# Order of transfers in one DMA queue of an adjacency-masked attention kernel: key factors and output transposes ahead of the probabilities' transposes

## What is computed

```
h    = relu(layernorm(x))                       # 4096 x 512
q    = h @ Wq.T + bq;  k = key @ Wk.T + bk;  v = value @ Wv.T + bv
s    = (q @ k.T) / 64 * adj                     # 4096 x 4096
s    = where(abs(s) < 1e-5, -1e9, s)
out  = x + (softmax(s) @ v) @ Wm.T + bm
```

## Time and profile before

| what | value |
|---|---|
| median of three runs | 1658.34 us (1650.92, 1658.34, 1658.66) |
| the profiled execution | 1648.3 us, of which its span is 1646.5 us |
| PE busy | 1534.5 us, 93% of the span, 6998 matmuls |
| DVE busy | 1135.8 us, 69% |
| ACT busy | 649.8 us, 39% |
| DMA queue of SP | 305.74 MB, 71.9% of 16 engines' time |
| mean granted TensorE clock | 0.988 of full speed |

### The profile page before, as it was taken

One profiled execution on the slowest core, in us unless ns is written; L12 is line 12 of the kernel. 1 busy time (PEld: TensorE's weight loads), 2 busy tenths in 40 slices (PEclk: granted clock), 3 DMA queues, 4 the chain that ended last, 5 costly groups with the idle time before them and its releaser, 6 DMA issues.

```text
span 1646.5 us, 23808 instructions
## 1 busy us (share of the span) xinstructions
PE 1534.5 (93%) x6998; PEld 692.3 (42%) x6998; DVE 1135.8 (69%) x2295; ACT 649.8 (39%) x1080; POOL 217.1 (13%) x291
## 2 busy tenths in 40 slices
PE   8998999959999999898999989899998989989898
PEld 5543444424334444343444434344443434434344
DVE  5889777747777666585766768576676857667573
ACT  5866444323333333343333434333343433334332
POOL 6163000010010101001010100101001010100100
PEclk9999999979999999999999999999999999999999
DMA  9725777757877778696776768677677867768664
GB/s 347 259 60 121 197 193 179 176 156 173 195 189 189 214 180 192 192 203 188 179 196 184 198 193 208 181 178 189 183 199 198 199 177 177 189 186 195 188 144 103
DMA packets 470020, 306.50 MB, mean 186 GB/s; under 512 B 378307, under 2 KB 390851, under 8 KB 469830
## 3 DMA queue, kind: packets, MB, share of 16 engines
q1 hardware_dynamic: 469952, 305.74, 71.9%
q10 hardware_dynamic: 6, 0.01, 0.0%
HBM read 194.78 MB, written 19.40 MB: 130 GB/s over the span
## 4 chain that ended last, share of the span: by engine, by line
PE 71%; DMA 14%; DVE 6%; SPq 5%; issue 3%; ACT 2%; DVEq 0%; ACTq 0%
PE R L871 11%; PE R L872 11%; PE R L873 11%; DMA Kbuf<-key_factors 11%; PE S L871 9%; PE S L873 8%; PE S L872 8%; SPq L593 4%; PE M L871 3%; PE M L872 3%; PE M L873 3%; DMA ho<-row 1%; PE R L989 1%; DVE Zbuf L1657 1%; DMA key_factors<-early 1%
## 5 line engine op out<-in xcount | busy, mean ns | idle before, releaser
L1335 ACT ACTIVATE drop<-Zbuf 128x512 f32<-128x512 f32 x256 | 160.8, 628 | 663.3 <-DVE cmx L1657 351.5
L871 PE MATMUL R<-Vbuf,pT 128*128 128x512 f16 x1008 | 384.6, 382 | 4.9 <-DMA pT<-ph 2.3
L872 PE MATMUL R<-Vbuf,pT 128*128 128x512 f16 x1008 | 384.5, 381 | 0.0
L873 PE MATMUL R<-Vbuf,pT 128*128 128x512 f16 x1008 | 384.1, 381 | 0.0
L871 PE MATMUL S<-Kbuf,qT 128*128 128x512 f16 x628 | 239.9, 382 | 66.4 <-DMA Kbuf<-key_factors 66.0
L873 PE MATMUL S<-Kbuf,qT 128*128 128x512 f16 x628 | 240.2, 382 | 0.0
L872 PE MATMUL S<-Kbuf,qT 128*128 128x512 f16 x628 | 239.9, 382 | 0.0
L1713 DVE SCALAR_TENSOR_TENSOR Zbuf<-S,rs,adjb 128x512 f32<-128x512 f32 x145 | 108.5, 748 | 117.8 <-PE S L873 103.6
L1657 DVE CUSTOM_DVE_ANT_0 Zbuf<-drop,Zbuf 128x512 f32<-128x512 f32 x256 | 183.7, 718 | 0.0
L1765 DVE TENSOR_SCALAR drop<-drop,common 128x512 f32<-128x512 f32 x232 | 135.8, 585 | 64.4 <-ACT drop L1335 62.2
L871 PEld LDWEIGHTS R<-Vbuf,pT 128*128 128x128 f16 x1008 | 98.8, 98 | 127.6 <-DMA pT<-ph 4.7
(11 more groups left out here) (277 smaller groups left out, 2048.0 us busy)
## 6 DMA issues: line engine op xcount, KB each, us to landing
Kbuf<-key_factors SPq DMA_DIRECT2D x171, 512.0 KB, 4.1
adjb<-in_adj_dram SPq DMA_DIRECT2D x256, 256.0 KB, 3.4
xq<-in_x_dram SPq DMA_DIRECT2D x32, 256.0 KB, 2.9
Kbuf<-in_L_gnn_key_dram SPq DMA_DIRECT2D x8, 1024.0 KB, 13.9
xr<-in_x_dram SPq DMA_DIRECT2D x32, 256.0 KB, 2.8
out_dram<-xr SPq DMA_DIRECT2D x31, 256.0 KB, 3.1
Vbuf<-in_L_gnn_value_dram SPq DMA_DIRECT2D x7, 1024.0 KB, 7.8
key_factors<-early SPq DMA_DIRECT2D x48, 128.0 KB, 2.4
```

Source lines behind the costliest of these rows:

```text
L871: nc.tensor.matmul(ps, lhs[0], rhs[0], start=start, stop=False, skip_group_check=added)
L872: nc.tensor.matmul(ps, lhs[0], rhs[1], start=False, stop=False, skip_group_check=added)
L873: return nc.tensor.matmul(ps, lhs[1], rhs[0], start=False, stop=stop, skip_group_check=added)
L1335: nc.scalar.activation(drop[:, :], tile_of(s.i, s.j), ACT.Abs).then_inc(abs_ready, 1)
```

## The change

In SP's `step` the inner loads move from behind the probabilities' transpose to ahead of it, and the transpose of a finished row's output moves from the end of the step to a place right behind the inner load. Each keeps its own waits. Nothing is added or left out on any engine. `turn_out` is the old text of the output's transpose as a function.

```diff
@@ -580,6 +580,14 @@
+            def turn_out(s, rows):
+                wait(sp, o_split, s.b - 1)
+                sp.sem_inc(split_seen, 1)
+                if s.has_next:
+                    wait(sp, qp_done, s.b + 2)
+                    sp.sem_inc(slot_seen, 1)
+                sp.dma_start_transpose(ho[:, :, :, :].rearrange("p h s n -> p (h s) n"), rows).then_inc(o_in, 16)
+
             def load_probs(s):
                 u = s.j - LAG_P
                 wait(sp, p_lo, s.t - LAG_P + 1)
@@ -603,15 +611,17 @@
                     sp.wait_ge(kt_stored, 16 * (2 * len(PIECES) if s.three else 32))
                     wait(sp, scores_done, s.t)
                     load_factor(*starts[s.j])
+                inner = INNER_THREE if s.three else INNER_TWO
+                if s.strassen and s.j in inner:
+                    if s.j == 4 or s.j == 6:
+                        wait(sp, unit_mm, 2 * s.before + s.j - 2)
+                    else:
+                        wait(sp, p1_mm, s.before + {2: 1, 3: 2, 5: 3}[s.j])
+                    load_factor(*inner[s.j])
+                if s.c == 4 and s.has_out and not last_out(s):
+                    turn_out(s, rows)
                 if s.early:
                     load_probs(s)
-                    inner = INNER_THREE if s.three else INNER_TWO
-                    if s.j in inner:
-                        if s.j == 4 or s.j == 6:
-                            wait(sp, unit_mm, 2 * s.before + s.j - 2)
-                        else:
-                            wait(sp, p1_mm, s.before + {2: 1, 3: 2, 5: 3}[s.j])
-                        load_factor(*inner[s.j])
                 if s.has_scores and s.more_adj:
 
                     wait(sp, z1_ready, s.t + 1)
@@ -627,13 +637,6 @@
...
-                if s.c == 4 and s.has_out and not last_out(s):
-                    wait(sp, o_split, s.b - 1)
-                    sp.sem_inc(split_seen, 1)
-                    if s.has_next:
-                        wait(sp, qp_done, s.b + 2)
-                        sp.sem_inc(slot_seen, 1)
-                    sp.dma_start_transpose(ho[:, :, :, :].rearrange("p h s n -> p (h s) n"), rows).then_inc(o_in, 16)
```

## The result

The changed kernel took 1591.74 us in the median of four runs (1588.81 to 1592.98), the kernel before 1654.72 beside it (1650.92 to 1658.66). The ratio is 0.9617 with a 95% interval of 0.9583 to 0.9651, so 3.8% faster. The forecast was 1596 us, with a range of 1576 to 1625. The profiled executions went from a span of 1646.5 to 1591.2 us, 55.3 us less, against a sum of 58.

The account below looks back on a forecast made before the run. PE was taken to be bound by 83.3 us of waits for key factors, mostly inner loads late in SP's queue. Gains of 55, 2.0 and 1 us sum to 58; 1654 - 58 = 1596 us, range 1576 to 1625.

Parts of the forecast that it names:

- a sum of 58: Total predicted gain in us: 55 from eleven passes with three units, 2.0 in pass 4, 1 in pass 3.
- The bound and the cause: PE waits 83.3 us for factors; in steps 3 to 6 inner loads are late by SP's queue order, not transfer length.
- the two gaps of pass 3: PE waits of 8.6 and 8.1 us, each ending with a first B11 whose load stays behind the transpose.
- What is late next: Steps 3 to 6: ACT's copies and DVE's sums limit the gain; 23.8 us a pass, 5.0 gained, eleven passes 55.
- all gaps close: Rival: DVE and ACT early enough, steps 3 to 6 fall to 21.3 us a pass, 87 us gained, 1567 us; chance 0.06.
- The output's transpose, costed at nothing: Moving 31 output transposes in SP's queue gains nothing, as PE reads `ho` only at the end of step 6.
- Passes 3 and 4: Pass 4 gains 2.0 us from its first two gaps, pass 3 gains 1 us from an earlier load.
- Head loads: Rival: T1 and B11 of steps 3 to 5, still behind transpose and tile, bind; 35 us lost, 1631 us; chance 0.10.
- Slower: transposes late: Rival: probabilities' transposes land late behind loads issued ahead, PE waits for `pT`; 1695 to 1849 us; chance 0.04.
- From the sum to the time: Starts from 1654 us, the average of four known times, not the profiled 1648.3, and subtracts 58: 1596 us.

Follow-up runs that it names:

- inner_alone_again: Against the kernel before, only the inner loads moved ahead, the output's transpose at its old place, on a second chip: 1601.56 us.
- full_again: The changed kernel, unaltered, run again on another chip: 1592.13 us.
- head_ahead: Changed kernel, plus the next step's head load ahead of the probabilities' transpose in passes with three units: 1591.91 us.
- sums_head: Changed kernel, plus two DVE low halves moved behind its sums and the next step's head load ahead of the probabilities' transpose: 1573.07 us.

## Why the prediction was right, point by point

**The bound and the cause.** Confirmed. The added products' factors were late by the queue's order. With the inner loads alone moved, the kernel fell to 1600 us and the waits for factors to 33.4 us. With the full change they fell from 83.3 to 22.0 us, 17.5 of these in the two gaps of pass 3 that the prediction had set apart.

**What is late next.** This step made the number. Predicted distances were 3.5, 7.4, 5.7 and 7.2 us; over passes 6 to 14 they measured 3.51, 7.39, 5.76 and 7.21 in the mean. Over all eleven passes the stretch took 23.72 us, predicted 23.8. Eleven passes gained 55.7 us (47.3 + 8.4 by the starts of step 3), predicted 55. That ACT and DVE set these distances is shown by taking them away in turn: 1592 with both, 1573 without DVE's part and the head loads behind it, 1565 without ACT's too. The rival "all gaps close" named 1567 for this. Of its conditions the prediction had the engines right, but it left out that the head loads must come earlier as well.

Part of the gain is the clock, as the prediction said. In five of the eleven passes of the kernel before, one of the four distances ran at a granted clock of 0.79 to 0.82, so in part at the lower level of 1.2 GHz; the earlier trace rows show one of them. Each came after a gap of 2.1 to 3.1 us. Other gaps of 2.0 to 2.3 us in these eleven passes had no lower clock behind them. From step 3 to B22 of step 6 the five took 29.7 us in the mean, the other six 28.0. By that the clock is worth up to 9 of the 55 us, an estimate from these means. In the changed kernel the stretch shows 1.00 in all eleven passes.

**The output's transpose, costed at nothing.** This term failed. It is worth about 9 us beside the inner loads and 0.4% alone, where the clock went with it. The prediction asked who waits for `ho` and what the transpose is moved ahead of. It did not ask what stood behind its old place: the head load of step 5, T1, which its product in step 6 then waits for. In pass 9 of the kernel before PE already waited for it, a fourth gap that the prediction's reading of steps 3 to 6 passed over:

```profile
971.67 0.39 PE L871 MATMUL S<-Kbuf 128*128 128x512 f16 x1 [0.50 <-DMA Kbuf<-key_factors]
```

Nor was `ho` early enough everywhere: two of PE's waits for it go with the move (`inner_alone_again` and `full_again`). The forecast did not suffer, because its 7.2 us for step 6 tacitly held that this load came early enough, and in the changed kernel it does.

**Passes 3 and 4.** Sized wrong: 3 us predicted, none found (0.4 us lost up to pass 5). For pass 4 the prediction took 3.5 us to B21 of step 3, from the end of ACT's copy in pass 9. In pass 4 the copy comes later, and PE waits for it in place of the factor:

```profile
471.63 0.39 PE L874 MATMUL S<-Kbuf,qT 128*128 128x512 f16 x1 [1.86 <-ACT Zbuf L1298]
```

Step 3 takes 5.33 us to B21 there, against 5.74 before. In pass 3 the gap that was to shrink by 1 us shrank from 8.10 to 7.56. The other grew from 8.6 to 9.93: its load goes out at 343.2 us in both kernels, but took 5.8 us to land in place of 4.5. Why it took longer was not tried.

**Head loads.** The prediction gave T1 about 4.8 us to land, and 0.8 more in which PE waits for DVE in any case, against a median of 4.1; it gave 0.10 to their binding at 1631. They came close to that limit: T1 of step 6 in pass 9 went out at 944.82 and PE took it up at 950.34, 5.5 us later, with 0.56 us of idle time (timelines of pass 9 above). The distance did not grow by it, 7.22 us against 7.21 where DVE's sum ended the wait. So 13 waits for factors are left, not two, and waits for L1695 sum to 11.8 us where 15 to 20 were expected. The total hardly moves, since either one alone holds PE about as long (`head_ahead`).

**Slower: transposes late.** PE's waits for `pT` went from 3.4 us in 4 to 4.2 in 5, the new one in pass 4. Even right behind a factor a transpose took 5.1 us, where the prediction priced 7.2.

**From the sum to the time.** 58 us predicted, 55.3 between the two spans. The average of four times, 1654, taken as the start, agrees with the 1654.72 measured later. Between the medians it is 63 us; as the prediction held possible, the kernel before spreads more than the changed one (1650.92 to 1658.66 against 1588.81 to 1592.98) and the granted clock rose from 0.988 to 0.992.

## What to carry to other kernels

Where transfers share one queue, look at each item's own release and at what stands behind it: an item that waits for a late engine holds up all that was ready, and one that is moved away can be worth its 1.24 us of queue time to the load behind it. Price such a move by retiming the stretch with the next-late engine's rows, not by the waits that vanish; here the waits for factors fell by 61 us and 55 were gained, part of that by the clock. When several releasers stand within a few tenths of each other, moving one alone can show nothing (`head_ahead`), and the same move pays when the others have gone (`sums_head`).

## What the hardware showed that was not expected

Two factors issued within 0.85 us of each other land later than apart. The list of DMA issues of the whole span, changed kernel:

```profile
Kbuf<-key_factors SPq DMA_DIRECT2D x171, 512.0 KB, 4.8
```

4.8 us in the median, where it was 4.1 for the same 171 loads before. Load by load in this trace, the 88 that have another within 1 us took 5.4 us in the median and the other 83 took 4.2. This is part of why the head loads came so close.

A transpose issued 0.7 us behind a factor took 5.1 us in pass 9 (`head_ahead` above). If the two landing times simply added up, it would have taken about 7.1 (4.7 - 0.7 + 3.1), so the two overlap. The Trainium skill ("DMA: Bandwidth & Descriptors", section on queues, rings and completion order) says that descriptors of one ring are consumed in order, but that a later one may finish its write before an earlier one. This trace agrees: of the 959 transfers of SP's queue all land in the order in which they are issued, but for one pair of weight loads at its start, where the later lands 0.6 us before the earlier. The transpose above landed at 934.0 us, about 1 us behind the factor at 932.9. All 45 transposes issued within 1 us behind a factor landed after it, in 5.0 us in the median and 6.4 at most. What these times do not bear out is the sum by which the prediction priced a transpose behind a factor, 7.2 us.
